# Four graph networks in one kernel: 22 tiles fewer in passes two and three, and a new order in the dense layers

## The reference

```python
edge_index = jnp.stack([src, dst])
x = _layernorm(x + _L0_gnn_ref(x, edge_index, ...))          # 4 layers: h = x + segment_sum(x[src], dst); two matmuls
x = _layernorm(x + _L1_gnn_ref(x, edge_index, edge_type_8, ...))   # per kind: mean over edges of (x @ W[r])[src]
x = _layernorm(x + _L2_gnn_ref(x, edge_index, edge_type_16, ...))  # sum over edges of alphas[rel] * (x @ w_rel[rel])[src]
x = _layernorm(x + _L3_gnn_ref(x, ..., src, dst, edge_type_8))     # sum over edges of gate * ((x @ W[rel])[src] + bias[rel])
```

## Time and profile before

| what | us |
|---|---|
| median of 3 runs (2251.11 to 2255.48) | 2252.14 |
| the profiled execution | 2252.56 |
| its span, first to last instruction | 2250.8 |
| setup, to the end of `adj` | 0 to 212 |
| dense layers, normalization, `tablex` | 212 to 669 |
| pass one | 669 to 1190 |
| pass two | 1190 to 1717 |
| pass three and the end | 1717 to 2251 |

### The profile page before, as it was taken

The page is one execution under the profiler, slowest core; times in us unless marked ns, Lnnn a source line. Parts: engine busy times, 40 slices in busy tenths (PEclk is TensorE's granted clock), DMA queues, the critical chain, the costliest instruction groups (busy, mean ns, idle before and its releaser), DMA issues.

```text
span 2250.8 us, 31616 instructions
## 1 busy us (share of the span) xinstructions
PE 1463.2 (65%) x7538; PEld 989.7 (44%) x7539; DVE 906.3 (40%) x2269; ACT 599.7 (27%) x1689; POOL 1360.4 (60%) x1574
## 2 busy tenths in 40 slices
PE   4776999999987777777764655555455433434433
PEld 2332554545456665666653533343333333323333
DVE  7887122213673444444445533333344212212212
ACT  3776000000023333333331644444343000000000
POOL 5000166720007777777777777777777777777775
PEclk8888999999988989989897876667677756565565
DMA  1000011100213333333333222222222222222221
GB/s 31 0 0 10 15 9 12 11 3 0 59 54 109 94 113 112 95 112 110 95 113 97 72 81 79 71 80 79 71 81 84 56 56 56 55 56 56 55 56 46
DMA packets 126652, 137.49 MB, mean 61 GB/s; under 512 B 80706, under 2 KB 97866, under 8 KB 123433
## 3 DMA queue, kind: packets, MB, share of 16 engines
q0 software_dynamic: 40896, 81.94, 13.9%
q1 hardware_dynamic: 85673, 54.54, 8.1%
HBM read 91.88 MB, written 44.52 MB: 61 GB/s over the span
## 4 chain that ended last, share of the span: by engine, by line
POOL 50%; PE 21%; issue 18%; ACT 5%; DVE 2%; ACTq 1%; DMA 1%; POOLq 1%; SPq 0%; DVEq 0%
POOL adj L1013 49%; PE acc L1315 18%; ACT adj L1714 5%; PE misc L1251 1%; PE acc L1586 1%; PE acc L1202 1%; ACTq L1707 1%; DVE adj L2607 0%; DMA adj<-table,adj 0%; DVE adj L2606 0%; ACTq L1714 0%; POOLq L1009 0%; PE acc L1251 0%; ACT adj L1773 0%; PE acc L1204 0%
## 5 line engine op out<-in xcount | busy, mean ns | idle before, releaser
L1013 POOL DMA_INDIRECT adj<-table,adj x832 | 793.5, 954 | 253.6 <-issue 252.9
L1586 PE MATMUL acc<-adj 128*128 x1760 | 364.5, 385 | 499.7 <-DMA adj<-table,adj 253.3
L1586 PEld LDWEIGHTS acc<-adj 128*128 128x128 f32 x1760 | 328.5, 285 | 560.3 <-issue 560.2
L1013 POOL DMA_INDIRECT adj<-tablex,adj x416 | 392.8, 944 | 210.9 <-issue 126.5
L1773 ACT ACTIVATE adj<-adj 128x128 f32<-128x128 f32 x832 | 264.5, 390 | 581.0 <-DMA adj<-tablex,adj 315.2
L1315 PE MATMUL acc<-adj,feat 128*128 (+1 forms) x2100 | 406.8, 354 | 8.4 <-issue 8.4
L1513 PE MATMUL acc<-adj 128*128 128x128 f32 x1664 | 245.3, 310 | 124.1 <-ACT adj L1773 113.9
L1997 DVE TENSOR_TENSOR adj<-acc,drel 128x768 f32<-128x768 f32 (+1 forms) x148 | 139.9, 948 | 423.6 <-PE acc L1586 423.3
L1513 PEld LDWEIGHTS acc<-adj 128*128 128x128 f32 x1664 | 228.8, 220 | 167.2 <-issue 167.1
L1315 PEld LDWEIGHTS acc<-adj,feat 128*128 (+1 forms) x2100 | 186.2, 98 | 217.1 <-issue 13.1
L959 POOL TENSOR_TENSOR node_rep<-node_rep,compb 128x128 f32<-128x128 f32 x128 | 58.5, 457 | 272.4 <-DMA node_rep<-in_L_gnn_weight_dram 263.5
(11 more groups left out here) (352 smaller groups left out, 1297.6 us busy)
## 6 DMA issues: line engine op xcount, KB each, us to landing
table<-adj SPq DMA_DIRECT2D x24, 1024.0 KB, 4.1
adj<-table,adj POOLq DMA_INDIRECT x834, 2.5
table<-adj SPq DMA_DIRECT2D x25, 512.0 KB, 2.9
adj<-tablex,adj POOLq DMA_INDIRECT x416, 2.5
table<-adj SPq DMA_DIRECT2D x25, 64.0 KB, 2.0
out_dram<-adj SPq DMA_DIRECT2D x24, 64.0 KB, 1.5
temp<-in_x_dram SPq DMA_DIRECT2D x4, 256.0 KB, 3.1
wrel<-node_rep SPq DMA_DIRECT2D x16, 64.0 KB
```

The source lines that it names most:

```text
L1013: pool.indirect_dma_start(ring[:, p_, 0:D], None, rows_, bass.IndirectOffsetOnAxis(ap=gidx[:, p_:p_ + 1], axis=0)).then_inc(msgs_in[third_ ...
L1586: last = nc.tensor.matmul(acc[:, bass.ds(blk[s], width)], hot[:, c, j, :], ring_flat[:, bass.ds(place[s], width)], start=False, stop=True, ...
```

## The change

In passes two and three one tile a turn is emptied, the eighth of the seventeen, in the 22 turns 2 to 23. Its 128 edges move to the places of 128 other edges of the same block, those that lead from a node to itself, and what these would have brought is added from the products that DVE has anyway. POOL's gather, ACT's scaling and PE's matmul of that tile fall away (`emptied`). Per block DVE adds 16 products, weighted by a one-hot of the kind, for pass two (`own_rows`, in pass one), one addition in pass two (`block_sum`), and 8 products for pass three (`table_parts`).

To find the self-edges and to fill their places, POOL does three lookups for each of 22 tiles (`found_rows`: a row of 16, a row of 8, a single word), and two scatters for each (`filled`), with DVE's steps `loop_nodes`, `loop_eighths`, `loop_holes` between. POOL and SP also write and read a few lists in DRAM. The setup loads one more list of destinations and marks self-edges, so that the count of repeated edges can tell where the scheme doesn't fit, and the program's other branch is taken then.

```diff
-EARLY_SLICES = (range(0, 6), range(6, 11), range(11, 16), ())
+EARLY_SLICES = (range(0, 4), range(4, 7), range(7, 13), range(13, 16))
...
+            sp.dma_start(next1_i[0:EVENQ, :], ...).then_inc(ends_in, 16)          # three loads
...
+            hold(sp, ends_in, ENDS_IN)
+            sp.dma_start(first_list, firsts_i).then_inc(ends_in, 16)
             sp.dma_start(compb[:, :, :], g2comp.partition_broadcast(P)).then_inc(comp_in, 16)
...
             with sp.Else():
+                sp.dma_start(eighths[0:TILES - 1, :]..., bass.AP(dst.tensor, dst.offset, [[P // 16, (TILES - 1) * (P // 8)], [1, 1]])).then_inc(ends_in, 16)
+                sp.wait_ge(late_counted, LISTS_SET)
+                for g in range(KINDS_OF_LIST):
+                    sp.dma_start(by_place(holes[g]), no_hole...).then_inc(ends_in, 16)
                 layers(False)
-                sp.wait_ge(edges_out, SWAPPED * 16)
-                sp.dma_start(moved[:, :, :], ...).then_inc(edges_in, 16)
...
+            pool.wait_ge(ids_in, 12 * 16)
+            nc.gpsimd.tensor_tensor(next1_i[:, :], next1_i[:, :], ids_i[:, 0, :], ALU.subtract).then_inc(before_set, 1)
...
-                    for j in range(SIZES[c]):
+                    for j in range(SIZES[c] - (1 if c == 1 and emptied(ph, u) else 0)):
                         p_ = place_of(ph, u, c) + j
                         pool.indirect_dma_start(ring[:, p_, 0:D], None, rows_, ...)
...
+                pool.wait_ge(late_counted, LISTS_SET)
+                pool.dma_start(edge_codes..., tile16[:, FROM_TILE:TILES]).then_inc(loops_in, 16)
+                for k, o in ((0, here_i), (1, behind_i)):
+                    pool.dma_start(o, bass.AP(dst.tensor, dst.offset + emptied_tile(0) * P + k, [[1, P], [TPT * P, LN], [1, 1]])).then_inc(edges_in, 16)
+                pool.wait_ge(ends_in, ENDS_IN + NONE_OUT)
+                pool.dma_start(firsts_b, first_list.partition_broadcast(P)).then_inc(edges_in, 16)
+                slices(0, 4)
+                pool.wait_ge(late_counted, NODES_SET)
+                found_rows(lambda b: sixteen[:, b, :], lambda b: eighths, row_i)
+                slices(4, 7)
+                pool.wait_ge(late_counted, EIGHTS_SET)
+                found_rows(lambda b: eight[:, b, :], lambda b: dst[0:E // 8 * 8]..., row_i)
+                slices(7, 9)
+                pool.wait_ge(late_counted, HOLES_SET)
+                found_rows(lambda b: found[:, b:b + 1], lambda b: edge_codes, row_i)
+                filled(0)
+                slices(9, 13)
+                filled(1)
+                pads()
+                for n in range(SWAPPED // 4):
+                    edges_part(n)
+                slices(13, 16)
                 passes(False)
...
+                for r in range(lo, hi):                                             # own_rows, DVE, pass one
+                        ins = nc.vector.scalar_tensor_tensor(mine, rows_, of_r, mine, ALU.mult, ALU.add)
```

More of the change, by code:

```diff
@@ L655, in tiles_from, with by_place, emptied, picks @@
             return u.num(TPT, PARTS_AT[c])
-        def msgs_before(ph, u, c):
-            uses = sum(uses_in(q, third_of(ph, u), c) for q in range(1, ph))
-            return u.third(16 * SIZES[c], 16 * SIZES[c] * uses)
+        def by_place(list_):
+            return list_.rearrange("(h p i) z -> p h (i z)", h=LISTS, p=P)
+        def emptied(ph, u):
+            return ph > 1 and (not isinstance(u.k, int) or LB <= u.num() < LB + LN)
+        def picks(b):
+            return not isinstance(b.k, int) or LB - 1 <= b.num() < LB + LN
+        def full_turns(r):
+            return sum(1 for i in (*range(LB), *range(LB + LN, TURNS)) if i % AHEAD_T == r)
+        def tiles_in_pass(ph, r, c):
+            n = uses_in(ph, r, c)
+            if ph == 1 or c != 1:
+                return n * SIZES[c]
+            return n * (SIZES[c] - 1) + full_turns((r - ph + 1) % AHEAD_T)
+        def msgs_upto(ph, u, c):
+            before = sum(tiles_in_pass(q, third_of(ph, u), c) for q in range(1, ph))
+            if ph == 1 or c != 1:
+                return u.third(16 * SIZES[c], 16 * (before + SIZES[c]))
+            full = full_turns(u.r) - (1 if u.r == (TURNS - 1) % AHEAD_T and not u.last() else 0)
+            return u.third(16 * (SIZES[c] - 1), 16 * (before + SIZES[c] - 1 + full))
         def uses_in(ph, r, c):
@@ L1769, in take @@
                     return
-                hold(act, msgs_in[third_of(ph, u)][c], msgs_before(ph, u, c) + 16 * SIZES[c])
-                for j in range(SIZES[c]):
+                hold(act, msgs_in[third_of(ph, u)][c], msgs_upto(ph, u, c))
+                for j in range(SIZES[c] - (1 if c == 1 and emptied(ph, u) else 0)):
                     o = ring[:, place_of(ph, u, c) + j, 0:D]
@@ L2285, in layers @@
                 for l in range(LAYERS):
+                    if l == 0 and not general:
+                        code_lists()
                     if l == 1 and not general:
@@ L2289, in layers @@
                         merge(l)
+                    if l == 1 and not general:
+                        loop_eighths()
                     if general:
@@ L2373, in body @@
                     if before.exists():
-                        table_parts(1, before)
+                        table_parts(1, before, now=False)
+                    own = before.exists() and picks(before)
                     if b.exists():
                         block_sum(1, t, b, False)
+                        if own:
+                            own_rows(before, 0, 4)
                         block_norm(1, b)
@@ L2459, in table_parts @@
                     nc.vector.tensor_copy(own, acc[:, SIDE_AT[1]:SIDE_AT[1] + D]).then_inc(prod_free[SIDE], 1)
+                    if not general and picks(b) and now:
+                        own_rows(b, 0, R2)
                 else:
```

331 lines of the change are left out of this document (284 added, 47 removed).

## The result

| | before | after |
|---|---|---|
| median, us | 2251.62 (2250.69 to 2255.48) | 2355.05 (2351.04 to 2357.71) |
| ratio, 95% interval | 1 | 1.0454 (1.0433 to 1.0476) |
| profiled execution, us | 2252.56 | 2357.25 |
| its span, us | 2250.8 | 2355.5 |

The change costs 103 us. Slower was forecast, with a chance of 0.87, but 2285 us was too low by 70 us, and the range ended at 2320.

The account below looks back on a forecast made before the run. POOL's gathers were taken as the bound of the passes, PE's dense layers ahead of them. On 2252.56 us: -55.4 gathers, +74 stall, +3 clock, +5 setup, +5 and +1 pass ends = +32.6, so 2285 us; range 2262 to 2320.

Parts of the forecast that it names:

- T: Dense layers: end of POOL's last weight slice, forecast at 303 + 347 = 650 us, bounds 642 to 660 us.
- I price each at the scatter's 1.27 us: POOL in the dense layers: 138 lookups and scatters at 1.27 us each, 175 us.
- DVE's steps at nothing: Dense layers: DVE's three steps feeding POOL's lookups cost nothing; one that is late adds its lateness to T.
- Element loads: Before POOL's first slice: two direct loads of 2,816 single elements, some 2.7 us each; high end 21 us each.
- The rival of dear loads: Element loads at their high end: POOL starts at 335 us, T = 682 us, time 2317 us; chance 0.13.
- Who waits for that: Layer 3: weight-list loads held on SP behind slices 13 to 15 make PE stand 74 us at L1406.
- TensorE's slower start: Behind PE's stall in layer 3: matmuls run at a reduced clock after the pause, 3 us more.
- Setup: Setup: three more index loads on SP, POOL's added subtraction and three more DVE operations, 5 us, bounds 3 to 9.
- The gathers and the ends of passes: Passes two and three: 44 fewer gathers save 55.4 us; DVE's products at the pass ends cost 5 and 1 us.
- DVE's work hardly slows the gathers: Rival for passes one and two: 590 added DVE operations slow gathers by 32 us, time 2317 us; chance 0.05.
- The passes did get shorter: Rival for passes two and three: another engine sets the pace, the 55 us don't come, 2340 us; chance 0.02.
- POOL is not early enough: Rival in the dense layers: POOL ends early enough, T = 617 us or less, even the quickest 2235 us; chance 0.10.

Follow-up runs that it names:

- all repairs: Change with loop codes 64 bytes apart, single-word transfer in setup, lists, x and first-table matrix loads ahead of slices 13 to 15, pads before second-half codes: 2227.04 us, 0.9885.
- the last experiment: Against the changed kernel, only loop codes 64 bytes apart and the single-word transfer in the setup; load order unchanged: 2293.08 us, ratio 1.0181 to before.
- the spread alone: Against the changed kernel, only each loop code put in 64 bytes of its own in DRAM: 2299.97 us, ratio 1.0212 to before.
- The kernel with the loads moved: Against the changed kernel, only SP's 13 loads of the layer-3 lists issued ahead of slices 13 to 15: 2308.59 us, ratio 1.0251 to before.

## Why the prediction was wrong

**What failed is T, the end of POOL's last slice:** forecast 650 and 5 us for the setup, measured 721.7. 56 of the 67 us are the two pauses (30.9 - 3.3 and 28.8 - 0.3 us), 8 are the later first slice (316.2 us, forecast 308), and 2 to 3 are spread over the chain. The step behind it was "I price each at the scatter's 1.27 us". For POOL that was right: the scatters of loop codes took 1.27 us each, and the lookups 1.25. But a scatter was priced by its issue alone, by a row of scatters of 16-byte rows to scattered places, as if what it does in DRAM cost nobody anything. With side-by-side words it cost the others that use DMA some 30 us a half. That the place of the words is the cause is shown twice: the pauses go when the words are moved apart in the change, and come back when they are put together again in the kernel with all repairs. From the first issue of a half to the end of its pause it is 52 and 49 us for 1,408 words; an estimate from these is 35 to 37 ns a word, if they drain all that time.

The Trainium skill, "DMA: Bandwidth & Descriptors", section "Specifications", gives 512 bytes as the least size of a transfer for full rate, with a read-modify-write below it. By size alone, words 8 to 64 bytes apart should have suffered like those side by side, since each is a transfer of 4 bytes. They didn't, so size alone is not what these runs show.

**What the pauses stop.** A transfer held up was shown (30.3 us for a slice's load). The engines came late, too: PE's matmuls come in short runs with gaps named "issue", POOL stood for 28.8 us between two scatters, and one issue on SP took 5.9 us where its like take 0.9. What held them is open. The Trainium skill, "Runtime: NRT & Kernel Launch", section "Instruction fetch mechanics", says that each engine streams its instructions by a DMA queue of its own, at a cost that is mostly hidden. The trace agrees that instructions come by DMA, and shows transfers of them slowed: two fall among the loop codes' scatters (at 520 and 620 us) and took 3.6 and 3.2 us, where the same two took 1.5 and 1.0 us with spread words. But none is on record within either pause, so no run shows that late instructions made them. For POOL's own pause a limit on its scatters in flight would do as well: in every trace with side-by-side words and the scatters to `holes` it stands ahead of the same scatter, the fourth of the edges. Against this, without the scatters to `holes` it stands ahead of its pads, which are no transfer.

**DVE's steps at nothing:** the code list "made ahead of the merge that stands at 288.3 us" was taken up by POOL at 304.7. The added transfer of single words, which the prediction didn't count, and the wait of 12.8 us beside it were not seen. Over the traces this wait is 7.6 to 13.1 us in the eight kernels with the transfer at this place and 3.6 to 3.7 us in the five with it in the setup, as in the kernel before. With the pauses away as well (the last experiment against the spread alone, by medians) moving it is worth 7 us. Whether single words do this or words that land side by side wasn't tried: no run writes those of `eighths` apart.

**Element loads:** right, at the low end. The two loads of 2,816 elements took 2.76 us together, 1.38 each, where 2.7 each was taken. The rival of dear loads is out.

**Who waits for that:** right. L1546 stalls behind a DVE chain that waits for lists that SP holds behind slices 13 to 15; in the last experiment, where the last slice ends at 651.5 us, the stall is 71.2 us, forecast 74. The kernel with the loads moved confirms it, by 46 us even with the pauses in it. TensorE's slower start was 1.5 us, forecast 3.

**Setup:** 5 was forecast; SP's x loads are at 271.96 us instead of 266.47, +5.5. The profiled executions of the variants had them at 270.3 to 276.6 us, so 4 to 10; see below.

**The gathers and the ends of passes:** 55.4 us less is right, with the mean duration unchanged at 954 ns and 12 us given back where 6 was forecast. At the change from pass one to two POOL waits 7.5 us (pass one up to there is 553.8 us long instead of 545.0, so 8.8 with what stands around it; forecast 5); at the change to pass three it waits 4.4 us (forecast 1, bound 5). There the argument that POOL "did not wait there for anything" in before took a row without a wait for a margin; how near the wait was no row said.

**The rivals.** DVE's work hardly slows the gathers: the mean is 954 ns as before in passes two and three, and in pass one, where most of the sums are, 949 ns instead of 944, which is 2 us over the pass and not 32; with the sums left out it is 944 again. The passes did get shorter. POOL is not early enough, though the kernel with all repairs ends near 2227, below that rival's 2235, by another way: not with POOL quicker, but with the lists and loads taken from behind it. That way was not among the rivals.

**The sums.** Two figures of the prediction are off by a little. Its bounds for T, setup and ends add up to 2273 to 2304 us and not 2272 to 2302, and two loads at 21 us instead of 2.7 put POOL's start at 340 us and that rival at 2322 us and not 2317, just outside the range. Neither changes this account.

## What to carry to other kernels

Price a scatter twice: by its issue, and by where its words land and what else uses DMA while they drain. Put a word of padding between small scattered words before any finer study. A load that others wait for should not stand behind the work of a slow engine on an in-order queue; before reordering there, list for each step what now covers it, since the same 28 scatters hid a load in one order and delayed the gathers in the other.

## What the runs showed of the hardware that was not expected

- 22 scatters of 128 four-byte words each, side by side in DRAM, cost 55 us in two pauses, and 33 us where lists and loads stand ahead of the last slices; the same words 8 bytes apart cost nothing that the time shows. What in the chip makes touching words so slow stays open. The scatters' own packets are on record while they are issued; in the pauses behind them 0 to 3 GB/s are moved, in the first with two transfers in flight.
- A transfer on one queue can delay an engine that neither issues it nor waits for it: 7.6 to 13.1 us on DVE with 6,640 single words issued some 15 us ahead, 3.6 to 3.7 us without. The words land side by side here as well.
- In the setup ACT stood for 12.6 us at 52 us into the span, with nothing to wait for, in eight of the fourteen traces (timeline of ACT in the kernel with all repairs below), and for 9.3 and 10.7 us in two more. In the other four, which are those of before, of after, of the words 16 bytes apart and of the last experiment, it waits at this place 5.7 to 8.0 us for PE. SP's x loads come at 276.1 us with all repairs and at 270.3 in the last experiment. This is the candidate for the 6 us between its runs: it, and the kernel with 16 bytes, were profiled in executions without the longer stall, and each was the fastest of its four. It was not tested.

```profile
52.28 0.59 ACT L1876 ACTIVATE adj<-acc 128x500 f32 x1 [12.58 <-issue]
```
